# Bank-aligned output pieces and VectorE-added routing bias in a fused mixing and expert kernel

## What is computed

```
h   = gelu(cond @ W0 + b0);  h = gelu(h @ W1 + b1)
att = softmax(h @ W2 + b2)
agg_w = einsum('bk,koi->boi', att, weight);  agg_b = att @ bias_k
y = einsum('boi,bih->boh', agg_w, x) + agg_b[:, :, None]
# per row of y (8192 rows of 1024):
logits = y @ W_router.T                 # 8 columns
top-2 of softmax(logits), weights normalised over the two
hA   = y @ A.T                          # 8 experts x 16 = 128 columns
out  = x + y @ W_base.T + b_base + 2 * (hA * combine) @ B
```

## Time and profile before

| | us |
|---|---|
| median of 3 runs | 944.49 (944.46 to 944.65) |
| the profiled execution | 944.94 |
| its span, first to last instruction | 943.3 |
| TensorE busy | 936.6 (99%) |
| VectorE busy | 773.8 (82%) |
| ScalarE busy | 476.4 (51%) |

### The profile page before, as it was taken

How to read it: one execution, slowest core, us unless ns; L and a number is a source line. 1 busy time by engine, 2 the same in 40 slices (tenths; PEclk the granted TensorE clock), 3 DMA queues, 4 the chain that set the end, 5 groups by cost and what they waited for, 6 DMA issues and landing times.

```text
span 943.3 us, 19762 instructions
## 1 busy us (share of the span) xinstructions
PE 936.6 (99%) x6687; PEld 932.7 (99%) x6687; DVE 773.8 (82%) x2327; ACT 476.4 (51%) x915; POOL 97.5 (10%) x139
## 2 busy tenths in 40 slices
PE   9999999999999999999999999999999999999998
PEld 8999999999999999999999999999999999999997
DVE  5986666888888888888888888888888888888876
ACT  6655454545454455454454555454545454545451
POOL 1130101100101100101010101001011001011010
PEclk9999999999999999999999999999999999999999
DMA  8444435343445343444344354444353434453434
GB/s 300 149 109 103 108 116 137 95 133 90 104 127 134 92 127 79 114 134 115 111 112 92 114 136 105 122 95 110 114 136 97 129 91 107 120 136 93 134 91 112
DMA packets 36055, 111.41 MB, mean 118 GB/s; under 512 B 13200, under 2 KB 13456, under 8 KB 31936
## 3 DMA queue, kind: packets, MB, share of 16 engines
q1 hardware_dynamic: 26656, 77.32, 22.5%
q0 software_dynamic: 9376, 33.78, 21.9%
HBM read 75.37 MB, written 35.65 MB: 118 GB/s over the span
## 4 chain that ended last, share of the span: by engine, by line
PE 97%; DMA 1%; DVE 1%; SPq 0%; issue 0%; ACT 0%; DVEq 0%
PE ps L446 25%; PE ps L444 25%; PE ps L442 25%; PE ps L509 9%; PE ps L478 4%; PE ps L476 4%; PE ps L480 4%; DMA w_stage<-in_wide 1%; PE ps L469 0%; PE ps L468 0%; PE ps L535 0%; DVE w_stage L1341 0%; SPq L381 0%; SPq L375 0%; DVE w_lo L1133 0%
## 5 line engine op out<-in xcount | busy, mean ns | idle before, releaser
L442 PE MATMUL ps<-w_hi,x_hi 128*128 128x290 f32 x1544 | 457.9, 297 | 0.4 <-DVE x_lo L1138 0.3
L446 PE MATMUL ps<-w_hi,x_lo 128*128 128x290 f32 x1544 | 458.0, 297 | 0.0
L444 PE MATMUL ps<-w_lo,x_hi 128*128 128x290 f32 x1544 | 457.8, 296 | 0.0
L442 PEld LDWEIGHTS ps<-w_hi,x_hi 128*128 128x128 f32 x1544 | 292.0, 189 | 2.4 <-DVE w_lo L1133 0.9
L444 PEld LDWEIGHTS ps<-w_lo,x_hi 128*128 128x128 f32 x1544 | 291.4, 189 | 0.0
L446 PEld LDWEIGHTS ps<-w_hi,x_lo 128*128 128x128 f32 x1544 | 291.1, 189 | 0.0
L1107 DVE STREAM_TRANSPOSE blocks_hwT<-hw 32x32 f32<-32x32 f32 x832 | 168.5, 203 | 25.3
L720 ACT CAST x_hi<-xT_sb 128x512 fp32r<-128x512 f32 x186 | 112.5, 620 | 29.9 <-DVE xT_sb L1038 22.2
L1022 DVE TENSOR_TENSOR x_lo<-xT_sb,x_hi 128x512 fp32r<-128x512 f32 x186 | 125.1, 686 | 0.7 <-ACT x_hi L720 0.7
L763 ACT COPY sum<-ps 128x580 f32<-128x580 f32 x96 | 62.0, 646 | 111.4 <-PE ps L446 111.4
L993 POOL DMA_DIRECT2D x_sb<-in_x x62 | 53.7, 867 | 510.5 <-ACT x_sb L744 495.0
(11 more groups left out here) (137 smaller groups left out, 1232.3 us busy)
## 6 DMA issues: line engine op xcount, KB each, us to landing
xT_sb<-in_xT SPq DMA_DIRECT2D x31, 1024.0 KB, 4.9
x_sb<-in_x POOLq DMA_DIRECT2D x62, 512.0 KB, 5.4
result<-x_sb SPq DMA_DIRECT2D x62, 512.0 KB, 2.7
b_sb<-in_wide SPq DMA_DIRECT2D x4, 580.0 KB, 13.6
agg_w_rows<-agg_w SPq DMA_DIRECT2D x1, 2048.0 KB, 7.5
mix<-agg_w_rows SPq DMA_DIRECT2D x124, 16.0 KB, 2.5
w_stage<-in_wide SPq DMA_DIRECT2D x4, 290.0 KB, 5.3
w_stage<-in_wide SPq DMA_DIRECT2D x2, 580.0 KB, 8.3
```

What stands on the lines that cost most here:

```text
L442: nc.tensor.matmul(dst, x_hi[:, s, rows], high[:, c, cols], start=first, stop=False, skip_group_check=True)
L444: nc.tensor.matmul(dst, x_hi[:, s, rows], low[:, c, cols], start=False, stop=False, skip_group_check=True)
L446: mm = nc.tensor.matmul(dst, x_lo[:, s, rows], high[:, c, cols], start=False, stop=last, skip_group_check=True)
```

## The change

CUTS becomes (0, 136, 648, 1160). The first piece now holds exactly the routing columns, and the 1024 output columns are two full banks of 512. So mixed(side, k) has 136, 512 and 512 columns, and the expert products touch two banks (OUT_PIECES = 1, 2) with 6 matmuls a tile. The first bank is no longer seeded: ScalarE has one seed of 1024 columns, the mixing matmuls start that bank afresh, and VectorE adds the bias as it takes the 136 columns out. Before mixed(side, 0) TensorE waits for hw_done of the tile before, in place of head_put. The result is one add of 1024 columns. head_put and head_out are gone. In unit_1, z12_low(1) is moved ahead of make_s3(2) and x_low(2, "A11"). In the last unit the pieces follow suit.

```diff
-CUTS = (0, 384, 772, WIDE)
-PIECES = 3
+CUTS = (0, AR, AR + BANK, WIDE)
+OUT_PIECES = (1, 2)
...
 def out_columns(piece):
-    first = max(CUTS[piece], AR)
-    return slice(first - AR, CUTS[piece + 1] - AR), slice(first - CUTS[piece], CUTS[piece + 1] - CUTS[piece])
+    return slice(CUTS[piece] - AR, CUTS[piece + 1] - AR)
...
             def mix_upper(u):
                 pe.wait_ge(mix_lo_done, tile_no(u, 0) + 1)
                 pe.wait_ge(z11_lo_done, u + 1)
-                pe.wait_ge(head_put, tile_no(u, 0) - 1)
-                mixed(0, 0, start=False).then_inc(ar_mm, 1)
+                pe.wait_ge(hw_done, tile_no(u, 0))
+                mixed(0, 0).then_inc(ar_mm, 1)
                 pe.wait_ge(z12_lo_done, u + 1)
                 pe.wait_ge(rest_put, tile_no(u, 0) - 1)
                 mixed(0, 1, start=False)
...
             def mix_lower(u, seeded=True):
                 pe.wait_ge(mix_lo_done, tile_no(u, 1) + 1)
                 pe.wait_ge(z22_lo_done, u + 1)
+                pe.wait_ge(hw_done, tile_no(u, 1))
+                mixed(1, 0).then_inc(ar_mm, 1)
                 if seeded:
-                    pe.wait_ge(head_put, tile_no(u, 1) - 1)
+                    pe.wait_ge(rest_put, tile_no(u, 1) - 1)
                 else:
                     pe.wait_ge(out_done, tile_no(u, 0) + 1)
-                mixed(1, 0, start=not seeded).then_inc(ar_mm, 1)
-                if seeded:
-                    pe.wait_ge(rest_put, tile_no(u, 1) - 1)
                 mixed(1, 1, start=not seeded)
...
             def expert_part(stat, mov, banks):
-                for k in range(PIECES):
-                    res, at = out_columns(k)
-                    mm = nc.tensor.matmul(ps[:, banks[k], at], stat[:], mov[:, res], start=False, stop=True,
+                for k in OUT_PIECES:
+                    mm = nc.tensor.matmul(ps[:, banks[k], :], stat[:], mov[:, out_columns(k)], start=False, stop=True,
                                           skip_group_check=True)
...
                 act.wait_ge(tile_bias_done, t - 1)
-                act.wait_ge(head_out, t)
-                nc.scalar.activation(ps[:, O_BANK, 0:width(0)], col_sum[:, columns(0)], ACT.Copy,
-                                     scale=tile_bias[:, side:side + 1]).then_inc(head_put, 1)
                 act.wait_ge(out_done, t)
...
-            def route(u, side, seeded=True, bank=O_BANK):
+            def route(u, side, bank=O_BANK):
...
-                if seeded:
-                    nc.vector.tensor_copy(ar[:, logits], ps[:, bank, logits]).then_inc(routed, 1)
-                    dve.wait_ge(routed, step + 1)
-                    nc.vector.tensor_copy(ar[:, lora], ps[:, bank, lora]).then_inc(routed, 1)
-                else:
...
+                nc.vector.scalar_tensor_tensor(ar[:, logits], col_sum[:, logits], agg_b[:, bass.ds(t, 1)],
+                                               ps[:, bank, logits], ALU.mult, ALU.add).then_inc(routed, 1)
+                dve.wait_ge(routed, step + 1)
+                nc.vector.scalar_tensor_tensor(ar[:, lora], col_sum[:, lora], agg_b[:, bass.ds(t, 1)],
+                                               ps[:, bank, lora], ALU.mult, ALU.add).then_inc(routed, 1)
...
                 dve.wait_ge(out_mm, t + 1)
-                res, at = out_columns(0)
-                nc.vector.tensor_tensor(x_sb[:, side, res], ps[:, O_BANK, at], x_sb[:, side, res], ALU.add
-                                        ).then_inc(head_out, 1)
-                rest = x_sb[:, side, res.stop:D].rearrange("p (k n) -> p k n", k=2)
-                nc.vector.tensor_tensor(rest, ps[:, O_BANK + 1:O_BANK + 3, out_columns(1)[1]], rest,
-                                        ALU.add).then_inc(out_done, 1)
+                out = x_sb[:, side, :].rearrange("p (k n) -> p k n", k=2)
+                nc.vector.tensor_tensor(out, ps[:, O_BANK + 1:O_BANK + 3, :], out, ALU.add).then_inc(out_done, 1)
...
                 result(0, 1)
+                z12_low(1)
                 make_s3(2)
                 x_low(2, "A11")
-                z12_low(1)
                 x_low(2, "A12")
...
             mixed(1, 1, LAST_BANKS[1], last_z_hi, last_z_lo)
-            expert_piece(0, 0, O_BANKS[0]).then_inc(last_piece_mm, 1)
             expert_piece(0, 1, O_BANKS[1], True)
             expert_piece(0, 2, O_BANKS[2], True)
...
-            for k in range(PIECES):
+            for k in OUT_PIECES:
                 expert_piece(1, k, LAST_BANKS[k]).then_inc(last_piece_mm, 1)
...
-            add_piece(1, 0, LAST_BANKS[0])
             add_piece(1, 1, LAST_BANKS[1]).then_inc(out_done, 1)
             add_piece(1, 2, LAST_BANKS[2]).then_inc(out_done, 1)
```

More of the change, by code:

```diff
@@ L230, in build @@
         tile_bias_done = sem("tile_bias_done")
-        head_put = sem("head_put")
         rest_put = sem("rest_put")
-        head_out = sem("head_out")
         mix_hi_done = sem("mix_hi_done")
@@ L425, in _ @@
             sp.dma_start(out_tiles[tile_no(LAST, 0)], last_x[:, 0, :]).then_inc(stored[0], 16)
-            last_cols = [slice(0, out_columns(1)[0].stop), out_columns(2)[0]]
-            for n, cols in enumerate(last_cols):
+            for n, k in enumerate(OUT_PIECES):
+                cols = out_columns(k)
                 sp.wait_ge(out_done, tile_no(LAST, 1) + 1 + n)
@@ L520, in expert_piece @@
             def expert_piece(side, k, bank, start=False):
-                res, at = out_columns(k)
-                dst = ps[:, bank, at]
+                res = out_columns(k)
+                dst = ps[:, bank, :]
                 pe.wait_ge(hwT_hi_done, tile_no(LAST, side) + 1)
@@ L1200, in unit_1 @@
                 z21_low(0, b)
-                route(0, 0, False)
+                route(0, 0)
                 dve.wait_ge(b_hi_done, 1)
@@ L1215, in unit_1 @@
                 make_s4(1)
-                route(0, 1, False)
+                route(0, 1)
                 x_low(1, "S4")
@@ L1307, in _ @@
                                     ).then_inc(z21_lo_done, 1)
-            route(u, 0, False)
+            route(u, 0)
             dve.wait_ge(p5_saved, u)
@@ L1331, in _ @@
             sum_half(0)
-            route(u, 1, False, LAST_BANKS[0])
+            route(u, 1, LAST_BANKS[0])
             sum_half(1)
@@ L1338, in add_piece @@
             def add_piece(side, k, bank):
-                dve.wait_ge(last_piece_mm, side * PIECES + k + 1)
-                res, at = out_columns(k)
-                return nc.vector.tensor_tensor(last_x[:, side, res], ps[:, bank, at], last_x[:, side, res], ALU.add)
+                dve.wait_ge(last_piece_mm, side * len(OUT_PIECES) + k)
+                res = out_columns(k)
+                return nc.vector.tensor_tensor(last_x[:, side, res], ps[:, bank, :], last_x[:, side, res], ALU.add)
             dve.wait_ge(x_in[0], u * 16 + 16)
-            add_piece(0, 0, O_BANKS[0])
             add_piece(0, 1, O_BANKS[1])
```

## The result

| | before | after |
|---|---|---|
| median, us | 944.57 (944.46 to 944.79, 4 runs) | 954.53 (953.98 to 954.67, 4 runs) |
| ratio, after to before | | 1.0104, 95% interval 1.0087 to 1.0122 |
| the profiled execution | 944.94 | 954.56 |
| its span | 943.3 | 952.9 |

The change makes the kernel 10.0 us slower, by its medians. The forecast was 949.2, 4.7 slower, with a range that ended at 952.8. The sign was right, the size was half of what came.

A forecast was written before the change was run, and what follows sets the result against it. TensorE's matmul starts were taken as the bound. Products +5.1 us, one stall -0.6 and the end +0.2 summed to +4.7, for a median of 949.2 us; range 947.0 to 952.8, forecast's chance 77%.

The forecast's parts named there:

- (4): VectorE: a 1024-column add takes 1.14 us; z12_lo is in time for mix_upper's second piece by 0.05 us; cost 0.
- (2): Mixing products cut 136, 512, 512: 110 ns from each 136, 229 ns per 512, so +114 ns a tile.
- rival A: Weight loads hide within the 70 ns of a 136, so mixing blocks stay as long: 941.5 us; chance 6%.
- B: Weight loads behind the 136s hide in part, 90 ns instead of 110: 945.4 us; chance 6%.
- (1): Expert products: six matmuls of 512 columns at 227.5 ns replace nine a tile, -35 ns a tile.
- a sign of being wrong: The prediction counts as wrong if a 512 costs under 226 or over 232 ns, or a short-matmul load isn't 110.
- (6): TensorE's new wait on hw_done ahead of the first mixing piece is always met: cost 0.
- Rival C: z12_lo comes late for mix_upper's second piece; some 29 units lose 0.1 us each, +3: 952.2 us; chance 10%.
- (3): Unit 1: TensorE's 0.57 us stall on z_lo goes because z12_low(1) moves ahead of two steps: -0.6 us.
- (5): ScalarE: two seeds become one of 1024 columns, 1.11 us against 1.48, starting later but hidden by 0.9 us cover: 0.
- (7): The end: a last add of 512 columns and a store grown from 194 to 256 KB cost +0.2 us together.

The follow-up runs named there:

- head_piece_232_wide: The changed kernel, with the three matmuls of the first mixing piece streaming 232 columns instead of 136, the extra ones unused: 953.36 us, ratio 1.0092.
- before_cuts_264_712: The kernel before with only its cuts moved to 264 and 712, giving expert pieces of 128, 448 and 448 columns: 954.24 us, ratio 1.0104.
- cuts_alone_all_seeded: The changed kernel with its seed part undone: ScalarE seeds the 136 columns too, TensorE waits for head_put, VectorE copies without bias: 951.55 us, ratio 1.0083.
- before_z12_first_unit1: The kernel before with only z12_low(1) moved ahead of make_s3(2) and x_low(2, A11) in unit_1: 944.23 us against 944.28, ratio 1.0001.
- before_unit1_and_even_stores: The kernel before with z12_low(1) first in unit_1 and the last tile's two stores cut at column 512: 943.62 us against 944.25, ratio 0.9990.
- rest_wait_first: The changed kernel with TensorE's rest_put wait in mix_upper moved from between the first and second piece to ahead of the first: 951.61 us, ratio 1.0074.
- z12_first_all_units: The changed kernel with z12_low(u) ahead of make_s3 and x_low(A11) on VectorE in every unit: 951.79 us, ratio 1.0076.

## Why the prediction was half right

- **The bound** was read rightly: TensorE's starts decide, and ScalarE's and VectorE's savings are worth nothing. ScalarE's two seeds of 904 and 580 ns became one of 1120 (L750, 60 of them, 67.2 us where the earlier trace rows have 89.0), 21.8 us less in the sum of the records, for 22 foretold. Records of neighbouring instructions overlap, though, and ScalarE's busy time on the page fell by 12.2 only (476.4 to 464.2). The 1024-column add takes 1.14 from start to start (477.25 to 478.39), as (4) had it.
- **Step (2), the weight load**: 110 ns from each 136 to the next start was right to the last digit that the rows have, and head_piece_232_wide and before_cuts_264_712 show that it is a floor. The page of the Trainium skill (TensorE: Matmul & The Clock Gate, section Back-to-back issue gap) has about 81 ns for 128 columns; this case's runs disagree with it for these fp32r operands, in two different blocks. Rivals A and B fall. A matmul under the floor costs the floor; the 70 ns that rival A needed is seen nowhere.
- **Steps (1) and (2), the pace of a 512**: the term that was mis-sized most. I divided what a matmul takes beyond 0.417 ns a column into 13 ns of its own and a part that grows, and took values between. The slope was in my rows (from 290 to 388, 0.45 a column), and it was the whole answer: 177 and 124 columns at 0.45 are 232.8, and 232.0 and 232.6 ns were measured where I took 227.5 and 229. A matmul less saves 5 ns, not 13: three less in the experts brought 8 ns a tile, not 35. The mixing block came out 21 ns above the forecast, and its 1590 of before, read from one block, is 1582.5 on average. Together -8 + 143 = +135 ns a tile for +79 foretold: 64 x 0.056 = 3.6 us of the 5.3 that were missing. My bounds had 232 in them; +8 us was written down as the upper end and given too little chance. The 232.6 is also over the 232 that the prediction named as a sign of being wrong.
- **Step (4)**: z12_lo was timed exactly. It was worked out to end 3.37 us behind the product's start (476.23 against 472.86); it ends at 480.35, 3.37 behind 476.98. Its margin was thinner than the 0.05 worked out: the load before starts at 480.30, so the next was due at 480.41, and 0.04 behind z_lo's end is 480.39. It would have been enough, as cuts_alone_all_seeded and units 2 to 4 show.
- **Steps (6) and (4) together** are where the reasoning failed. "The new wait is always met: 0" is true of the wait and false of the edit. Its value differs from that of the wait it replaces, and so a register instruction moved behind z12_lo's wait and ate the margin: 26 x 0.07 = 1.8 us. The sum had nothing for what stands in the queue between a wait and the matmul. Rival C had the place and nearly the count and size (29 units, 0.1), but its trigger, a late z12_lo, didn't occur.
- **Step (3)**: right in the trace (1.72 in the changed kernel's unit 1, 1.59 in before_z12_first_unit1's, for 2.15); the 0.6 us were too small to be seen in the time of the latter.
- **Step (5)**: right. In the profile after, no matmul waits for a seed.
- **Step (7)**: the sign was wrong. I let the larger store cost up to 0.3; the end became 0.6 shorter. 256 KB lands in 2.6 us and 194 KB in 3.3. before_unit1_and_even_stores shows it in the kernel before, so it belongs to the cut and not to something else of the change. It isn't the size, for 208 and 224 KB land in 2.7 and 2.5. What sets the cut at column 636 apart is open.

The miss, then: +3.6 for the pace of a 512, +1.8 for the register instruction, -0.8 for the end, and +0.4 for the start of the profiled execution: 5.0, where its span was 4.9 over the 948.0 foretold. Without the register instruction, the cuts cost 951.55 less 944.25, 7.3 us, with unit 1's reordering and the shorter end in it.

What stays open: the 290s. Their mean distance (191 to 880 us) is 134.2 ns before and 134.3 after the change, 134.0 in cuts_alone_all_seeded, rest_wait_first and z12_first_all_units, and 134.5 in before_cuts_264_712. All of them together take 727.0 us after and 726.3 to 726.4 in those three, 0.6 to 0.7 less, which is part of why these gain 2.4 to 2.9 us on the change where 1.8 is the stall. head_piece_232_wide has the stall and 726.3, so the stall isn't its cause. Nor do these runs tell why a column takes 0.444 ns at a granted clock of 2.4 GHz, where 0.417 would be one cycle.

## To carry to other kernels

Cut a product so that no piece falls under the width at which a weight load hides (some 237 columns here, for fp32r operands), even at the price of pieces that don't line up with the banks: a short piece costs as much as one of 237 columns, and a matmul saved is worth 5 ns. Take the price of a new width from a line through two measured widths, not from the clock and a constant. And where a wait ends last with hundredths to spare, look at what the queue has behind it: here each of two instructions in that place cost about 0.07 us, and a wait whose value is a new expression of the loop variable brings an instruction that stands where the value is first used, so put such waits ahead of the tight one.

## What was not expected of the hardware

- From 128 to 232 columns an fp32r matmul of this kernel costs the same, 110 ns from start to start.
- Above that, 4.6 + 0.444 N ns for N columns, from 256 to 512.
- A register instruction of 32 ns behind a wait that just ends held the next weight load up by 0.06 us and the block by 0.06 to 0.08; one instruction more, with two waits that were long met, cost the block 0.07 to 0.09 again.
- The last store of 256 KB lands in 2.6 to 2.8 us, of 208 and 224 KB in 2.7 and 2.5, of 194 KB in 3.2 and 3.3.
